# A mixture of experts on TensorE: two experts' weights side by side, products of 512 columns

## What is computed

```python
def _route_combine_weights(x_addr, U, k, tau):
    z = x_addr @ U.T
    topv, topi = jax.lax.top_k(z, k)
    w = jax.nn.softmax(topv / (tau + EPS), axis=1)
    ...
    return jnp.zeros((N, L), z.dtype).at[rows, topi].add(w)

def _mixture(inp, C, W):
    y = jnp.zeros((inp.shape[0], W.shape[1]), inp.dtype)
    for e in range(L):
        y = y + C[:, e:e + 1] * (inp @ W[e].T)
    return y
...
C1 = _route_combine_weights(xa, U1, K_ROUTE, TAU)
C2 = _route_combine_weights(xa, U2, K_ROUTE, TAU)
C3 = _route_combine_weights(xa, U3, K_ROUTE, TAU)
h = jax.nn.gelu(_mixture(xf, C1, W1), approximate=False)
y = _mixture(h, C2, W2) + C3 @ b2
```

## Time and profile before

| | |
|---|---|
| median of 3 runs | 3035.03 us (3033.9 to 3042.45) |
| the profiled execution | 3023.01 us, span 3021.2 us, mean granted clock 0.955 |
| PE busy | 2738.9 us, 91% of the span, 23816 matmuls |
| PEld busy | 2297.6 us, 76% |
| DVE busy | 2202.1 us, 73%, 5944 instructions |
| ACT busy | 1039.7 us, 34% |
| POOL busy | 820.5 us, 27% |
| DMA engines | 327.31 MB, mean 108 GB/s |

### The profile page before, as it was taken

The page is one execution under the profiler, slowest core; times in us unless marked ns, Lnnn a source line. Parts: engine busy times, 40 slices in busy tenths (PEclk is TensorE's granted clock), DMA queues, the critical chain, the costliest instruction groups (busy, mean ns, idle before and its releaser), DMA issues. The chain is left out here.

```text
span 3021.2 us, 61482 instructions
## 1 busy us (share of the span) xinstructions
PE 2738.9 (91%) x23816; PEld 2297.6 (76%) x23816; DVE 2202.1 (73%) x5944; ACT 1039.7 (34%) x1524; POOL 820.5 (27%) x858
## 2 busy tenths in 40 slices
PE   2599999999999999999999999999999999956886
PEld 1388888888888888888888888888888888736775
DVE  2467888887888887888888888888888888733332
ACT  1223433333334333333333333333333333211111
POOL 1000122222222222222222222222222222334334
PEclk7599999999999999999999999999999999967998
DMA  6633444443333333333333333333333331117785
GB/s 196 183 87 97 114 124 111 116 116 110 108 96 89 100 100 100 94 86 94 100 95 94 100 89 100 98 89 83 97 99 100 99 90 43 40 39 211 207 213 126
DMA packets 321183, 327.31 MB, mean 108 GB/s; under 512 B 45405, under 2 KB 302231, under 8 KB 320892
## 3 DMA queue, kind: packets, MB, share of 16 engines
q1 hardware_dynamic: 287100, 304.20, 35.6%
q0 software_dynamic: 33792, 19.17, 3.6%
HBM read 182.18 MB, written 212.37 MB: 131 GB/s over the span
## 5 line engine op out<-in xcount | busy, mean ns | idle before, releaser
L653 ACT ACTIVATE exps<-second 128x1024 f32<-128x1024 f32 x512 | 525.9, 1027 | 785.0 <-PE second L1135 777.1
L548 POOL DMA_INDIRECT expert_slots<-row_mem,sidx x512 | 509.1, 994 | 790.9 <-PE first L1117 553.8
L1215 PE MATMUL mixp<-w_h,r_part_h 128*128 128x256 f32 x3072 | 668.5, 299 | 40.1 <-DVE hid L906 24.0
L822 DVE TENSOR_REDUCE nm<-first 128x4 f32<-128x1024 f32 x512 | 623.2, 1217 | 93.1 <-PE first L1117 93.0
L1215 PE MATMUL mixp<-w_h,r_part_l 128*128 128x256 f32 x3072 | 609.7, 280 | 0.0
L1215 PE MATMUL mixp<-w_l,r_part_h 128*128 128x256 f32 x3072 | 609.3, 279 | 0.0
L1215 PEld LDWEIGHTS mixp<-w_h,r_part_h 128*128 128x128 f32 x3072 | 467.4, 189 | 97.0 <-DVE hid L906 31.7
L1215 PEld LDWEIGHTS mixp<-w_l,r_part_h 128*128 128x128 f32 x3072 | 468.4, 188 | 0.0
L1215 PEld LDWEIGHTS mixp<-w_h,r_part_l 128*128 128x128 f32 x3072 | 468.1, 188 | 0.0
L906 DVE SCALAR_TENSOR_TENSOR x_mem<-mixp,C,x_mem 128x256 f32<-128x256 f32 x768 | 329.6, 477 | 114.6 <-PE mixp L1215 114.2
L906 DVE SCALAR_TENSOR_TENSOR hid<-mixp,C,hid 128x256 f32<-128x256 f32 x704 | 300.7, 474 | 35.8 <-PE mixp L1215 33.8
(11 more groups left out here) (211 smaller groups left out, 3687.0 us busy)
## 6 DMA issues: line engine op xcount, KB each, us to landing
kst<-k_parts SPq DMA_DIRECT2D x256, 192.0 KB, 3.8
qst<-q_parts SPq DMA_DIRECT2D x256, 192.0 KB, 4.1
q_parts<-nat_h SPq DMA_DIRECT2D x128, 256.0 KB
k_parts<-ctx_part_h SPq DMA_DIRECT2D x64, 256.0 KB, 2.4
k_parts<-nat_h SPq DMA_DIRECT2D x64, 256.0 KB, 2.4
q_parts<-nat_l SPq DMA_DIRECT2D x64, 256.0 KB
exps<-in_wgu SPq DMA_DIRECT2D x39, 384.0 KB, 4.4
expert_slots<-row_mem SPq DMA_DIRECT2D x8, 1284.0 KB, 12.5
```

The costliest lines, as they stand in the source:

```text
L548: pool.e.indirect_dma_start(out=slots_dram, out_offset=bass.IndirectOffsetOnAxis(ap=sidx[b % 2][:, t, k:k + 1], axis=0), in_=row[b % 2][:, ...
L653: act.e.activation(exps[:, j % NU, :, :, :].rearrange("p k t s -> p (k t s)"), second[:, :, :].rearrange("p k s -> p (k s)"), ACT.Exp, sca ...
L822: dve.e.tensor_reduce(nm[u % 2][:, :, 2 * j:2 * j + 2].rearrange("p t k -> p k t"), first[:, :, :].rearrange("p k (t s) -> p k t s", t=TIL ...
L1215: m = pe.e.matmul(mixp[q % 2][:, t * D:(t + 1) * D], src[i][:, dt, t * P:(t + 1) * P], wmix[n][j][:, l, dt, :], start=(k == 0), stop=(k == ...
```

## The change

In memory, the weights of experts 2p and 2p + 1 now lie side by side: for each half of the features 512 columns, the first 256 those of expert 2p. A unit is now one tile through two experts. Unit i of a mixture is pair i // 2 and tile i % 2, so there are still 24 units in a batch, at the same places. TensorE makes six matmuls of 512 columns instead of twelve of 256, and the bank holds the two experts' results of one tile. VectorE's two operations of a unit go to the same tile, one after the other: the first waits for unit q - 2, the second for the first. The chunks of weights are the same pairs of experts with the same bytes in another order, and the host's reordering follows.

```diff
-    L = w1T_in.shape[1]
+    L = 2 * w1T_in.shape[1]
...
-        wmix = [[sb(f"w{n}_{p}", (P, L, DT, D), F32R) for p in "hl"] for n in (1, 2)]
+        wmix = [[sb(f"w{n}_{p}", (P, L // 2, DT, 2 * D), F32R) for p in "hl"] for n in (1, 2)]
...
-            for l in range(0, L, 2):
-                chunks.append(([w[:, l:l + 2, :, :].rearrange("p l a b -> p (l a b)") for w in wmix[n]],
-                               src[:, l:l + 2, :, :].rearrange("p l a b -> p (l a b)"), 2 * DT * D))
+            for pair in range(L // 2):
+                chunks.append(([w[:, pair, :, :].rearrange("p a b -> p (a b)") for w in wmix[n]],
+                               src[:, pair, :, :].rearrange("p a b -> p (a b)"), 2 * DT * D))
...
-                    b, n, l = a
-                    q = 2 * L * b + n * L + l
+                    b, n, i = a
+                    pair, t = divmod(i, TILES)
+                    q = 2 * L * b + n * L + i
                     dve.wait_ge(t_mix, q + 1)
-                    for t in range(TILES):
-                        acc = (hid if n == 0 else X[b % NXB])[:, t, :]
-                        src = mixp[q % 2][:, t * D:(t + 1) * D]
+                    acc = (hid if n == 0 else X[b % NXB])[:, t, :]
+                    for k in range(2):
+                        l = 2 * pair + k
+                        src = mixp[q % 2][:, k * D:(k + 1) * D]
...
                             if l == 0:
                                 dve.wait_ge(v_b2, 2 * b + t + 1)
+                            elif k == 0:
+                                dve.wait_ge(v_mix, 2 * (q - 1))
                             else:
-                                dve.wait_ge(v_mix, 2 * (q - 1) + t + 1)
+                                dve.wait_ge(v_mix, 2 * q + 1)
...
-                    pe.wait_ge(v_w, FIRST + n * (L // 2) + l // 2 + 1)
+                    pe.wait_ge(v_w, FIRST + n * (L // 2) + pair + 1)
...
-                    for t in range(TILES):
-                        k = 0
-                        for i, j in TERMS:
-                            for dt in range(DT):
-                                m = pe.e.matmul(mixp[q % 2][:, t * D:(t + 1) * D], src[i][:, dt, t * P:(t + 1) * P],
-                                                wmix[n][j][:, l, dt, :], start=(k == 0), stop=(k == 3 * DT - 1))
-                                k += 1
+                    k = 0
+                    for i, j in TERMS:
+                        for dt in range(DT):
+                            m = pe.e.matmul(mixp[q % 2][:, :], src[i][:, dt, t * P:(t + 1) * P], wmix[n][j][:, pair, dt, :],
+                                            start=(k == 0), stop=(k == 3 * DT - 1))
+                            k += 1
```

More of the change, by code:

```diff
@@ L1357, in mixture_rows @@
         n, o, i = w.shape
-        return np.ascontiguousarray(w.transpose(0, 2, 1).reshape(n, i // P, P, o).transpose(2, 0, 1, 3))
+        return np.ascontiguousarray(w.transpose(0, 2, 1).reshape(n // 2, 2, i // P, P, o).transpose(3, 0, 2, 1, 4)).reshape(
+            P, n // 2, i // P, 2 * o)
     def expert_rows(w, p):
```

## The result

The changed kernel takes 3088.4 us (median of 4 runs), the kernel before beside it 3037.5; the ratio is 1.017, 95% interval 1.0151 to 1.0189. It is 52 us slower, where 33 us less was forecast, and lies outside the range of 2958 to 3050. The profiled execution has a span of 3085.1 us.

What follows compares the result with a forecast made beforehand. TensorE was taken to set the pace in the middle (388.7 of 400 us busy); 88 us saved less 55 lost in waits gave 33, so 3035 - 33 = 3002 us, range 2958 to 3050.

Steps and rivals of the forecast that it cites:

- Part 1: TensorE's mixture: 4608 products of 512 columns at 0.216 us replace pairs costing 0.235, saving 88 us in all.
- rival 2: TensorE's mixture: 512 fp32r columns cost 0.235 us, nothing saved, VectorE's lateness remains; 3062 us, up to 3119; chance 0.15.
- Part 2: VectorE's two additions of a unit become dependent: 0.11 us more per unit, 84 us of VectorE in all.
- The semaphore rule: VectorE chains take the same time with a semaphore after each operation as one at the end; forecast some 27 us lower.
- Part 3: TensorE's waits for VectorE: 55 of the 88 us not gained, 28 lost savings and 27 VectorE's lateness; gain 33.
- four places, each with its count: TensorE's waits at unit 2 (10 us), units 8 and 7 (22), row maxima (14) and scores (9), together 55 us.
- The clock, SP, POOL, the chunks: Parts put at nothing: weight chunks, SP and POOL unchanged; the slow-clock head at most 2 us.
- Rival 3: No change: VectorE bounds the whole first mixture, waits cost 80 to 95 us against 88; say 3033 us; chance 0.13.
- Rivals 1 and 4: Full gain, VectorE's slack absorbing lateness, 2947 to 2975 us, chance 0.15; VectorE the only bound, near 2670 us, chance 0.02.

Runs made afterwards that it cites:

- e3_prices: Kernel before, with runs of 24 equal products of several widths and types appended behind its end, other engines at rest; 3117.5 us in one run.
- e5_one_wait: Kernel before, 256-column products, VectorE's second addition of a unit waiting for the first by one wait replacing its own; 3082.2 us, ratio 1.0155.
- e4_472: Changed kernel with mixture products of 472 instead of 512 columns, VectorE's operations unchanged; 3077.8 us, ratio 1.0137.

## Why the prediction was wrong

**Part 1, the price of the product: wrong, and it decided the sign of TensorE's term.** The step that failed is the one from the fp32 rows to the fp32r product. The excess of 0.0095 us at 256 columns was put down to the weights' load, because the product of 64 fp32 columns costs as much. Both numbers were right and the link between them was not: with 16 columns of weights 256 columns still cost 0.116 us, and 512 still 0.231. What stands above 0.108 is the fp32r column's own price of 0.456 ns against 0.42 for bf16. The rows of fp32 were misread besides: as `e3_prices` shows, an fp32 product stands in the trace as two records, so each eight of the earlier trace rows are four products, and their 0.84 ns a column belongs to one record and says nothing on what an fp32r column costs. I gave 0.235 as the upper bound and chose the lower one by a row that was near in length and load, but not in type. The mixture's own products said 0.117 at 256 columns, whatever stood around them, and rival 2 held that none of the rows proves a cheaper column. (Its "all" goes too far: the scores' products on 48 partitions at L1117 start 0.083 us apart, four from 1007.88 to 1008.21 us. They are of another kind than the mixture's, with two banks in turn.) Measured 0.234: saving 0 instead of 88 us. The Trainium skill (TensorE: Matmul & The Clock Gate, Back-to-back issue gap) gives N / 2.4 + 2.5 ns for a lone product, 216 ns at 512 columns. The bf16 row of `e3_prices` agrees with it, though it is a stream with a load beside each product (0.216 us); the fp32r row doesn't (0.233).

**Part 2, the dependent pair: right in mechanism, a tenth too small.** Forecast 0.11 us a unit, measured 0.12 (1.00 against 0.88 us); VectorE's busy time rose by 60 us where about 55 were named. The semaphore rule that was weighed there (the Trainium skill, VectorE: DVE Perf Modes, The DRAIN you can't avoid) would have made this part free; here a wait for the operation in front cost 0.12 us each time, and the kernel 47 us (`e5_one_wait`).

**Part 3, how much arrives: wrong by two in both directions.** Of VectorE's lateness 27 us were to arrive, 47 to 52 did. Of TensorE's saving two thirds were to arrive, three tenths did, and one tenth with VectorE late. The failed step is "four places, each with its count": it took the waits that existed and priced them, and left out the slack that was short without being zero. Of the 27 us, 15.5 were for `hid` (units 2, 7 and 8), 6.9 for the row maxima and 4.5 for the scores. `e5_one_wait` shows 11.5 for `hid` (both its lines), 20.8 for the maxima, whose waits rose from 63 to 92, 0.9 for the scores, and 13 at the two waits for `misc` that were not in the sum. So the places in the first mixture were priced well, the maxima at a third, and the second mixture cost more (27) than the first (21). After the change itself `hid` is waited for 86 times instead of 57. The average said 85% for VectorE and read as room; the runs say that both engines already held each other, since 98 us off VectorE alone gave 28.

**The clock, SP, POOL, the chunks:** nothing, as forecast; the granted clock in the middle is 0.99 to 1.00 in both kernels.

**The rivals.** Rival 2 came, at 0.15: the price of 512 columns at 0.234 (it named 0.235), TensorE gaining nothing and the lateness remaining. Its 3062 us had the lateness of part 3 in it; with the measured one it is 3088. Rival 3 had the other half of the truth (part 3 at 2.5 to 3 us a batch, 80 to 95 us in all): `e4_472` shows that with the cheap product it would have been even worse than that, 42 us slower. Rivals 1 and 4 had nothing for them. What would show it was named in the main: starts at 0.235 for rival 2, and the second addition 0.03 us behind the first. TensorE's waits for `hid` grew to 57 us and not to 70, those for the maxima by the 20 named. Its idle time, at 19 of 400 us, lay below the 24 set for rival 3 while the time already told of it; idle time of one engine alone doesn't measure this.

## What to carry to other kernels

A price is taken over only from an instruction of the same type: measure the new width once in a quiet tail before building on it. When two engines are both above some 80% and tied by waits in a fixed order, a microsecond on either is worth a part of a microsecond (here 0.3 to 0.6, and 0.1 on TensorE while VectorE was late), and a change that takes from one and gives to the other is a loss unless it takes far more than it gives. Two additions in a row into the same tile cost 0.12 us more than two into different ones; keep neighbours independent. And before the cost of a dose is read from a time, compare the granted clock of the two runs by stretch: here most of what looked like a dearer wait was a slower TensorE (some 65 of 85 us).

## What the runs showed of the hardware

- Fp32r products cost 0.451 to 0.456 ns a column from 256 columns up (0.117, 0.173 and 0.233 us at 256, 384 and 512), and at 256 and 512 the same within 0.002 us with 16 or 128 columns of weights. Bf16 cost 0.216 us at 512. 128 fp32r columns cost 0.110 us beside a load of 128 columns of weights.
- An fp32 product stands in the trace as two records of 0.429 us at 512 columns, so it costs 0.858 us, 3.7 times the fp32r product.
- A VectorE addition on 256 columns that waits for the one before starts 0.12 us later than one that doesn't (pairs of 1.00 against 0.88 us). With a second wait on the same operation a pair takes 1.07 us.
- The kernel with that second wait was 132 us slower, and its granted clock in the middle was 0.97 where the kernel before has 0.99 to 1.00. At the lower level an fp32r product of 256 columns cost 0.215 us (L1108), at the full one 0.117.
